# Where VectorE's statistics, the tokens of o and the entry to attention stand in the order of a macaron layer on one core

## The reference

```python
x = x + 0.5 * ffn(layernorm(x))
x = x + attention(layernorm(x))        # 16 heads of 8
x = x + 0.5 * ffn(layernorm(x))        # the same weights again

def ffn(x):                            # hidden size 512
    h = silu((x @ w1.T) * w1_s) * ((x @ w2.T) * w2_s)
    h = gelu((h @ h1.T) * h1_s)
    h = gelu((h @ h2.T) * h2_s)
    return (h @ w3.T) * w3_s
```

## Time and profile before

| | us |
|---|---|
| median of 3 runs | 622.78 |
| lowest, highest | 621.61, 626.68 |
| the profiled execution | 622.23 |
| its span, first to last instruction | 620.3 |

### The profile page before, as it was taken

The page is one execution under the profiler, slowest core; times in us unless marked ns, Lnnn a source line. Parts: engine busy times, 40 slices in busy tenths (PEclk is TensorE's granted clock), DMA queues, the critical chain, the costliest instruction groups (busy, mean ns, idle before and its releaser), DMA issues.

```text
span 620.3 us, 12783 instructions
## 1 busy us (share of the span) xinstructions
PE 589.7 (95%) x4452; PEld 437.2 (70%) x4452; DVE 442.0 (71%) x1048; ACT 466.3 (75%) x794; POOL 95.4 (15%) x258
## 2 busy tenths in 40 slices
PE   2989999999999999999999999999999999999996
PEld 1768878788676666665656565666678878788784
DVE  6885756958646777988979798896575756955742
ACT  4657877968874568787887888787787877968963
POOL 2072020022010312222223222012010020020000
PEclk9999999999999889999999999999999999999999
DMA  8300000000060343452617163400000001000011
GB/s 272 92 1 1 1 2 0 1 0 0 2 241 31 137 137 138 137 189 85 229 59 260 69 205 123 152 2 1 2 1 1 1 1 35 0 22 11 1 34 36
DMA packets 36693, 42.02 MB, mean 68 GB/s; under 512 B 2464, under 2 KB 27296, under 8 KB 36640
## 3 DMA queue, kind: packets, MB, share of 16 engines
q1 hardware_dynamic: 36640, 41.31, 19.8%
HBM read 22.42 MB, written 18.87 MB: 67 GB/s over the span
## 4 chain that ended last, share of the span: by engine, by line
PE 65%; DVE 10%; issue 9%; ACT 9%; POOL 3%; DMA 2%; SPq 1%; POOLq 0%; DVEq 0%; ACTq 0%
PE bank L1083 36%; PE bank L1191 7%; PE bank L1166 6%; PE bank L1178 3%; DVE act_lo L822 3%; DVE silu L831 2%; ACT silu L542 2%; PE bank L1180 2%; DVE neg_max L872 2%; PE bank L1223 2%; ACT act_hi L557 2%; PE bank L1148 1%; PE bank L1152 1%; ACT act_hi L534 1%; PE bank L1209 1%
## 5 line engine op out<-in xcount | busy, mean ns | idle before, releaser
L1083 PE MATMUL bank<-act_hi,WH 128*128 128x512 f32 x576 | 230.2, 400 | 4.3 <-DVE act_lo L822 1.2
L1083 PE MATMUL bank<-act_lo,WH 128*128 128x512 f32 x576 | 225.7, 392 | 0.0
L872 DVE TENSOR_REDUCE neg_max<-bank 128x2 f32<-128x512 f32 x256 | 166.3, 680 | 32.7 <-PE bank L1166 31.6
L842 DVE TENSOR_TENSOR act_lo<-full,act_hi 128x512 fp32r<-128x512 f32 x128 | 91.1, 713 | 111.4 <-ACT act_hi L557 111.2
L672 ACT ACTIVATE probs<-bank 128x512 f32<-128x512 f32 x256 | 139.3, 597 | 36.4 <-PE bank L1180 34.6
L555 ACT ACTIVATE full<-bank,SG 128x512 f32<-128x512 f32 x128 | 88.2, 689 | 68.7 <-PE bank L1083 67.9
L1083 PEld LDWEIGHTS bank<-act_hi,WH 128*128 128x128 f32 x576 | 108.2, 188 | 32.4 <-ACT act_hi L557 4.4
L1083 PEld LDWEIGHTS bank<-act_lo,WH 128*128 128x128 f32 x576 | 108.3, 188 | 22.6 <-issue 0.5
L1178 PE MATMUL bank<-QK 32*128 32x256 f32 x512 | 94.1, 333 | 0.6 <-ACT probs L672 0.4
L557 ACT ACTIVATE act_hi<-bank,SG 128x512 fp32r<-128x512 f32 x128 | 87.3, 682 | 0.0
L1180 PE MATMUL bank<-m_parts,SEL 32*128 32x256 f32 x512 | 80.2, 279 | 0.0
(11 more groups left out here) (95 smaller groups left out, 594.4 us busy)
## 6 DMA issues: line engine op xcount, KB each, us to landing
qk_scratch<-qk SPq DMA_DIRECT2D x64, 256.0 KB, 2.6
QK<-qk_scratch SPq DMA_DIRECT2D x16, 1024.0 KB, 7.1
raw_rest<-w_ffn SPq DMA_DIRECT2D x4, 512.0 KB, 6.6
out<-X SPq DMA_DIRECT2D x4, 512.0 KB, 3.2
X<-x SPq DMA_DIRECT2D x3, 512.0 KB, 7.5
raw<-w_ffn SPq DMA_DIRECT2D x3, 256.0 KB, 4.8
X<-x SPq DMA_DIRECT2D x2, 256.0 KB, 3.0
WA<-w_att SPq DMA_DIRECT2D x1, 256.0 KB, 5.1
```

Of the source, the lines that this page charges most:

```text
L842: D.tensor_tensor(act_lo[1 + layer][:, j, t, :], full[:, t, :], act_hi[1 + layer][:, j, t, :].bitcast(F32), op=ALU.subtract)\
L872: D.tensor_reduce(neg_max[:, bb, qt, n0:n0 + 2], bank[(banks or A_BANKS[bb])[u]][:, :].rearrange("p (h k) -> p h k", h=2), axis=AX.X, op=A ...
L1083: ins = MM(dst, a, b, start=k == 0, stop=k == len(todo) - 1)
```

## The change

1. `TOKENS` becomes (11, 13): the tokens of o at step 11 in even batches, with `norm_o` and `scale_o` at steps 12 and 13.
2. VectorE's statistics in even batches: six pieces (the statistics in two halves) at steps 3, 4, 5, 7, 8 and 9, in place of five at steps 7 to 11. `normalise` in odd batches: tile 0 at step 3, tile 1 at step 4, tiles 2 and 3 at step 5.
3. First body of each feed-forward phase: ScalarE makes the last product's high part and loads Gelu's table ahead of the first hidden tile, VectorE makes the low part ahead of the statistics.
4. GpSimd's low parts of the weights: nine instructions of one chunk in place of five of up to two, begun one product later (`h_lo` at 8), those from the sixth weight chunk on each behind one more `act_lo`. TensorE's waits for them are split over the places that use them, in the branch not taken.
5. Entry: transposes of the second pair ahead of hidden layer 2, j = 0, its projections of Q and K between those tiles, `qk_full` at an address that is free by then; its V behind the output products and read by ScalarE at step 2 of batch 0 in place of step 9; two of the six late maxima behind the first residual; GpSimd clears V1 after its `max_again` and no longer before.

```diff
-TOKENS = 13
+TOKENS = (11, 13)
...
-        below_ring = sb("below_ring", [P, 1504], F32, att)
+        qk_full = sb("qk_full", [P, 2, 2 * SEQ], F32, att)
+        below_ring = sb("below_ring", [P, 1504 - 4 * SEQ], F32, att)
...
-            pool.wait_ge(h_lo, L1_TILES - 1)
-            for k in range(2, len(W_GROUPS)):
-                pool.wait_ge(w_hi, k + 1)
-                pool.tensor_tensor(part_of(WL, k), raw_of(k), part_of(WH, k).bitcast(F32), op=ALU.subtract)\
+            pool.wait_ge(h_lo, L1_TILES)
+            pool.wait_ge(w_hi, len(W_GROUPS))
+            for c in range(C_H1, W_CHUNKS):
+                if c >= C_H2:
+                    pool.wait_ge(g_lo, SLOTS + c - C_H2 + 1)
+                src = raw[:, c:c + 1, :] if c < W_RAW else raw_rest[:, c - W_RAW:c - W_RAW + 1, :]
+                pool.tensor_tensor(WL[:, c:c + 1, :], src, WH[:, c:c + 1, :].bitcast(F32), op=ALU.subtract)\
                     .then_inc(w_lo_rest, 1)
...
             low_parts(1)
             max_again(0, 0)
+            pool.wait_ge(out_mm, NB)
+            clear_v(1)
             norm_for(0)
...
-                    side = {0: last_product}
-                    if not first:
-                        side |= {1: lambda: output(before, 0), 2: lambda: output(before + 1, 1)}
+                    if first:
+                        last_product()
+                        load_table(ACT.Gelu)
+                        side = {}
...
-                    hidden(g + 2 * HT, 1, 0)
+                    hidden(g + 2 * HT, 1, 0, {0: lambda: x_to_sbuf(1, 6), 2: entry_q, 3: entry_k} if into_att else {})
...
-                    if u == 9 and v_pair is not None:
+                    if u == (9 if prev else 2) and v_pair is not None:
                         set_v(*v_pair)
...
+                    if first:
+                        product_lo(t1, L1_TILES - 1)
                     for step in steps[0:1]:
                         step()
...
-                            entry_max(10, 11, 12, 13, 14, 15)
+                            entry_max(10, 11, 12, 13)
                         residual(nb + 2 * i, 8 * i, 0)
+                        if into_att:
+                            entry_max(14, 15)
...
+                    even = dict(zip((3, 4, 5, 7, 8, 9), norm_steps(n, 4 * q, 4, halves=True)))
+                    odd = {u: lambda t=t, w=w: normalise(n, 4 * q + t, t, w, last=t == 2)
+                           for u, t, w in ((3, 0, 1), (4, 1, 1), (5, 2, 2))}
...
+                    if into_att:
+                        pe.wait_ge(x_added, nb + 2 * i - 1 + CREDIT)
+                        transpose_att(1, 4, 6)
                     hidden(g + 2 * HT, 1, 0, g_lo, g + HT + SLOTS, general,
-                           {1: lambda: entry(0), 2: lambda: entry(1, 2), 3: lambda: entry(3)} if into_att else {})
+                           {1: lambda: entry(0), 2: entry_q, 3: entry_k} if into_att else {})
...
                         output(nb + 2 * i, 0, g + 3 * HT, general)
                         if into_att:
-                            pe.wait_ge(g_hi, NP * HID_TILES + CREDIT)
-                            transpose_att(1, 4, 4)
-                            entry(10, 11)
+                            entry(10, 11, 12, 13)
                         output(nb + 2 * i + 1, 1, g + 4 * HT, general)
+                        transpose_y(nb + 2 * i, 0)
                         if into_att:
-                            project_q(1, 5)
-                            entry(12, 13)
-                            project_k(1, 4)
                             entry(14, 15)
-                        transpose_y(nb + 2 * i, 0)
+                            pe.wait_ge(g_hi, NP * HID_TILES + CREDIT)
+                            project_v(1, 4)
                         transpose_y(nb + 2 * i + 1, 1)
...
-                    if u == TOKENS and own and prev:
+                    if u == TOKENS[bb] and own and prev:
```

More of the change, by code:

```diff
@@ L713, in att_body @@
             def att_body(i, par, ahead=True, more=True, first=False):
-                attend(2 * i, 0, prev=not first, prev2=not first, v_pair=(i + 1, 1 - par) if more else None)
+                attend(2 * i, 0, prev=not first, prev2=not first,
+                       v_pair=(i + 1, 1 - par, 4 if first else 6) if more else None)
                 attend(2 * i + 1, 1, prev2=not first, ahead=i + 2 if ahead else None)
@@ L922, in first_step @@
                     def first_step():
-                        product_lo(t1 + L1_TILES * i, L1_TILES - 1)
+                        if not first:
+                            product_lo(t1 + L1_TILES * i, L1_TILES - 1)
                         for step in steps[1:2]:
@@ L1017, in _, with attend @@
             ffn_phase(0)
[L1019 removed]
+            def attend(b, bb, prev=True, prev2=True, more=True, side={}):
                 for u in range(UNITS):
@@ L1111, in hidden @@
                 pe.wait_ge(ready_sem, ready)
+                if general and layer == 1:
+                    pe.wait_ge(w_lo_rest, C_W3 - C_H1)
                 xs = inputs_of(layer, j)
@@ L1344, in attend @@
                             pe.wait_ge(m_lo, b + 1)
+                            if not prev:
+                                pe.wait_ge(x_added, NB + CREDIT)
                         if v < UNITS:
@@ L1393, in att_body @@
             def att_body(i, par, ahead=True, more=True, first=False):
-                attend(2 * i, i, par, 0, prev=not first, prev2=not first, v_pair=i + 1 if more else None)
+                attend(2 * i, i, par, 0, prev=not first, prev2=not first,
+                       v_pair=i + 1 if more and not first else None)
                 attend(2 * i + 1, i, par, 1, prev2=not first, more=more, ahead=i + 2 if ahead else None)
```

89 lines of the change are left out of this document (49 added, 40 removed).

## The result

| | before | after |
|---|---|---|
| median | 622.19 (4 runs) | 631.68 (4 runs) |
| lowest, highest | 621.30, 626.68 | 629.41, 632.39 |
| the profiled execution | 622.23 | 631.55 |
| its span, mean granted clock of TensorE | 620.3, 0.99 | 629.7, 0.982 |

The kernel after takes 1.0122 times as long as the one before, 95% interval 1.0076 to 1.0167: slower by 1.2%. The forecast was 625.8 us with a range of 618.0 to 629.5, and "within 1%" as the likeliest case. The medians alone are 9.49 us apart. The result is 2.2 us outside the range.

A forecast was written before the change was run, and what follows sets the result against it. TensorE, busy 95% of the span, was taken to bound the kernel. Terms -2.4 + 1.2 - 0.5 + 3.65 + 1.6 = +3.55 us on 622.23 gave 625.8 us, range 618.0 to 629.5.

The forecast's parts named there:

- within 1%: Whole kernel: a result less than 6.2 us from no change, neither faster nor slower by that; chance 0.82.
- First body, -2.4: Phase 1's first body: TensorE's waits at the third hidden tile and at 41.46 go; 2.4 us saved, bounds 1.0 and 2.6.
- Entry, +1.2: Entry to attention: new 2.8 us wait for the first residual, partly given back; +1.2 us, bounds -0.7 and +1.7.
- I expect the clock to be low there again and the batch 0.5 shorter: Batch 0 without V's projection: clock again low, bound by latencies, 0.5 us saved.
- rival B: Clearly slower, 630 us: TensorE's 2.8 us hole at 181 halves the clock, costing 2.0 to 5.5 us more; chance 0.13.
- holes of about 1 us: Argument against rival B: such holes in the first body left the tiles behind them at 1.83 us.
- First odd batch, -0.5: At 230.43 TensorE waits 0.71 for a maximum behind four normalisations; pieces let it through, 0.5 us saved.
- they lie beside TensorE: VectorE's statistics: the same instructions, beside TensorE's work, so priced at nothing.
- Tokens at step 11, +3.65: Attention pairs: tokens moved to where TensorE is packed cost 0.53 in five pairs, 0.50 in two; bounds +0.7 to +4.2.
- 0.58 - 0.15: Per pair: 0.58 us for tokens at step 11 in the even batch, 0.15 back before the odd batch's first weighing.
- Rival A: Faster, 614.0 us: GpSimd's waits at the row maxima and the late normalisation are true costs; chance 0.12.
- First body of phase 2, +1.6: Phase 2's first body: Gelu's table load now follows the last product's copy, delaying the third tile; bounds +1.2 and +1.7.

The follow-up runs named there:

- b_f1: Kernel before with only the first body of phase 1 changed: 620.03 us, ratio 0.9953.
- a_res: Kernel after with VectorE's first residual of the entry moved behind the second act_lo: 625.55 us, ratio 1.0078.
- a_hole: Kernel after with eleven unread matmuls filling TensorE's wait for the first residual at 180.8: 633.00 us, ratio 1.0110.
- a_stat: Kernel after with statistics back at steps 7 to 11 and normalisation in one piece at step 3: 628.09 us, ratio 1.0076.
- a_tok13: Kernel after with the tokens of o back at step 13 in even batches: 626.05 us, ratio 1.0057.
- a_p2: Kernel after with the first body of phase 2 put back as before: 630.40 us, ratio 1.0121.
- a_best2: Kernel after with tokens at 13, statistics, normalisation and phase 2's first body as before, first residual early: 620.51 us, ratio 0.9947.
- a_fill: Kernel after with 6 unread matmuls in TensorE's holes before batch 0's first scores: 631.19 us, ratio 1.0143.
- a_best3: a_best2 with six unread matmuls in batch 0 and the normalisation in two halves: 619.74 us, ratio 0.9929.
- a_best4: a_best2 with the normalisation in two halves and V's projection of the second pair back at step 9 of batch 0: 617.38 us, ratio 0.9877.
- b_tok11: Kernel before with only the tokens of o at step 11 of even batches: 625.51 us, ratio 1.0052.
- b_f1_fill: b_f1 with 10 unread matmuls in TensorE's holes before batch 0's first scores: 619.81 us, ratio 0.9976.
- a_noentry: Kernel after with the entry to attention put back as before: 628.74 us, ratio 1.0100.
- b_best: b_f1 with the normalisation in two halves at steps 3 and 4: 619.82 us, ratio 0.9916.

## Why the prediction was wrong

**First body, -2.4:** right. It was -2.63 up to the first projection of Q, and b_f1's median is 2.9 below that of the kernel before on its chip.

**Entry, +1.2: the step that failed.** The wait was right to 0.1 us (2.8 predicted, 2.68 measured). The step that failed is the sentence "I expect the clock to be low there again and the batch 0.5 shorter": it took the half speed of the entry to be what it was before, in length and place, and left rival B's clock out of the sum. I had written down the mechanism and priced it: TensorE stands still for 2.8 us at 181 and the clock falls. I argued it away with holes of about 1 us, which were no row for a hole of 2.7. It cost 1.33 us there (a_res, a_hole). The larger part came where I had not looked: the stretch at half speed in batches 0 and 1 was 17.1 us instead of 10.2. By the profile of a_stat, with 6.8 us there, the long one costs 3.3 us up to batch 2 (the pieces, +0.4 in batch 0 and -0.5 in batch 1, nearly cancel in that comparison). Entry, first odd batch and clock together were +5.52, against +0.7: 4.8 us of a miss of 5.8. Of these 4.8, 1.33 are the clock at 181; the 6.9 us more of half speed than before are about 2.2 (an estimate: their share of the 10.2 us that cost 3.3); 0.4 are the pieces of the statistics in batch 0 (next paragraph). The other 0.9 have no run of their own.
A second comparison is a_stat with before: it stands at -0.37 us at the row maxima of batch 2, of which the first body is -2.6. So the entry is +2.3, and +0.9 without the 1.33 of clock at 181, against +1.2 (a_stat has the normalisation in one piece, so the -0.5 is not in it); but it has 6.8 us of half speed in the batches against 10.2, so this is no clean test.
How long the stretch lasts differs between executions of one kernel: the mean clock of before is 0.983 or less in 14 of 86, at 625 to 628 us. With the changed entry a mean clock of 0.985 or less is common: three of four in after, ten of eleven in a_tok13, four of four in a_p2, three of eight in a_stat, four of ten in a_res, three of four in a_hole, five of ten in a_best2; a_fill and a_best3, with matmuls in batch 0, and a_best4, with V's projection back there, have none of four, of seven and of four. With the old entry it is rare: one of ten in b_tok11 and b_f1_fill, one of seven in a_noentry, none of ten in b_f1 and in b_best. Only part of that is the 3.4 us at 181, which a_res, a_hole and a_best2 do not have. What in the entry does it stays open.
The Trainium skill (TensorE: Matmul & The Clock Gate, Part 1) says that the monitor of activity runs on its own and does not start with the kernel, so that the number of matmuls at the low clock varies from run to run. The page says it of a kernel's first matmuls. The traces agree in that the amount varies, here 200 us into the kernel: the same code had 10.2 us of it in one execution and 20.5 in another (before, b_tok11). That the monitor's own time is the reason, no run here shows.

**First odd batch, -0.5:** right. In after the half speed hides it, but other traces had the full clock in batch 1. Starts of the row maxima (transposes of neg_max) of batches 1 and 2, in before and in a_res:

```profile
226.09 0.44 PE L1201 MATMUL bank<-EYE,neg_max 128*128 128x128 f32 x2
241.26 0.44 PE L1201 MATMUL bank<-EYE,neg_max 128*128 128x128 f32 x2
```
```profile
223.38 0.44 PE L1221 MATMUL bank<-EYE,neg_max 128*128 128x128 f32 x2
238.03 0.44 PE L1221 MATMUL bank<-EYE,neg_max 128*128 128x128 f32 x2
```

| | stretch at half speed | maxima of batch 0 to 1 | of batch 1 to 2 |
|---|---|---|---|
| before, one piece | 212.0 to 222.5 | 14.81 | 15.17 |
| b_f1, one piece | 211.0 to 222.0 | 15.07 | 15.16 |
| a_best2, one piece | 212.0 to 219.5 | 14.02 | 15.15 |
| a_res, three pieces | 213.5 to 220.5 | 14.42 | 14.65 |
| a_noentry, three pieces | 209.5 to 223.5 | 16.31 | 14.65 |
| b_best, two halves | 212.5 to 220.0 | 14.11 | 14.65 |
| after, three pieces | 214.5 to 232.0 | 16.26 | 16.21 |

One piece takes 15.16, pieces or halves 14.65: 0.51 less. The pieces of the statistics in batch 0, which stood in the sum at nothing ("they lie beside TensorE"), seem to take 0.4 of it back: 14.42 in a_res, 14.02 in a_best2, both with 6.8 us at half speed.

**Tokens at step 11, +3.65:** right in mechanism, too small: +5.39, above its own upper bound of 4.2. The odd batch came out as walked: -0.25 for the delay that goes, +0.40 for `add_att`, +0.14 in all against +0.10. The mis-sized term is "0.58 - 0.15" for the even batch, which measured 0.70 (14.74 to 15.44): the steps ahead of the tokens, the chain behind them and the steps after the next weighing each ran 0.05 to 0.13 us longer than the spacings of the earlier trace rows. The 0.13 ahead of the tokens come with the pieces of the statistics, the other term at nothing: after and a_tok13 have them, b_tok11 doesn't. The first pair without statistics measured 0.71 against 0.50; by the forecast's own terms, 0.58 - 0.15, it should have been 0.43.
Rival A, that the waits for GpSimd and the normalisation in one piece are true costs, falls on its main leg: the waits went, and nothing came sooner. The other leg, the delay by the one piece, is real: 0.25 in a steady odd batch, 0.51 in the first.

**First body of phase 2, +1.6:** right in the trace (a wait of 1.51, the third tile 1.61 later than before after the last transposes of attention) and in a_p2, 1.55 less in its trace.

**The sum.** 3.55 predicted, 9.32 measured: clock and entry +4.8, pairs +1.7, the first body with the start -0.4, the rest -0.3. Rival B's mechanism came true, and that the total lies near its 630 is in part luck: it priced the half speed at 181 at 2.0 to 5.5 us, where it cost 1.33, and had neither the long stretch in the batches nor the 1.7 of the pairs. Its 4.2 "in the middle" is not the middle of its bounds either, which is 3.75. The range's upper end of 629.5 cut off most of B, as its own price of 4.2 on top of 625.8 shows. It should have reached 631.

## What to carry to other kernels

A wait that is new, and longer than any that the trace shows at full clock, is a wait plus a question about the clock; if rows show the clock falling after TensorE worked in pieces elsewhere in the same kernel, put that price in the sum and in the range. What half speed costs depends on where it falls: here some 0.2 us for each us at half speed in batch 0 and 0.39 in batch 1. Filling holes with empty matmuls kept the clock up and gained 1.4 to 1.5 us up to the next stage, and nothing in the medians; taking the wait away won 4 us. And a wait that a list names is worth nothing until the start behind it moves: compare the starts of the next work that matters (here the weighing), not the wait.

## What the runs showed of the hardware

Three of VectorE's four small instructions with one input from SBUF, of 8 columns, took 1.27 us instead of 0.15 beside GpSimd's low parts (37.47, 40.46 and 42.24 in after; the same three in b_f1). Each of the three ended within 0.03 us of the end of one of GpSimd's instructions; the fourth, at 38.66, took 0.15 and fell between two of them. I had expected the slowing only of those with two inputs. The statistics beside the same instructions of GpSimd were not slowed (8 in 1.64 us). The Trainium skill (VectorE: DVE Perf Modes, What auto-detection actually checks) says that the engine takes its 2×_2P mode if a single source and the destination are in SBUF and their outermost dimensions (those of one element aside) are both even or equal. That mode uses both ports. That these instructions ran in it and so waited for GpSimd fits the rows; no run here tests it.

Filling the wait of 2.7 us with matmuls kept the clock at 1.00 there, and 30 us later TensorE was at half speed all the same, for 24 us (a_hole).

Gelu started 1.65 us after its table load began in after (31.84, 33.49), 1.28 of it the load; no pause beyond the warming activation shows behind a load.
